# Around the first image pair of a whitening and Fourier-filter kernel: order of the mask products, banks of the inverse column transform, statistics of the second pair, idle products around the factor

## The chip, the cores and the metric

The kernel runs on one core of one Trainium2 chip. The metric is device time in microseconds (us), the median of several runs. Engines are named as in the profile: PE is the matrix engine, DVE the vector engine, ACT the scalar engine, POOL the general engine, SP the queue that starts transfers.

## The reference, cut to what matters

The input is `x`, 16 images of 56 x 56 positions with 64 channels, fp32. First a whitening over all positions, then one block of a Fourier network:

```python
f = x_flat - mean(x_flat); ff = (1-EPS) * f @ f.T / (n-1) + EPS * I      # 64 x 64
L = cholesky(ff); x = solve_triangular(L, I) @ f * gamma + beta
h = layer_norm(x, n1_g, n1_b)
xf = rfft2(h)                                   # per image, over both axes
o1 = relu(complex block product of xf with w1, + b1)   # 8 blocks of 8 channels
o2 = softshrink(complex block product of o1 with w2, + b2, 0.01)
h = irfft2(o2) + h + x
out = gelu(layer_norm(h, n2_g, n2_b) @ mw1 + mb1) @ mw2 + mb2 + h
```

## The kernel before

The 16 images are worked in 8 pairs; a pair is 112 rows (2 images x 56) by 3584 values. The instructions of each engine are one list in a fixed order, written out by hand, with semaphores between the engines.

**Head, once.** `covariance` builds the 64 x 64 Gram matrix from all pairs as they arrive. `factor` eliminates it column by column: 63 steps that go PE to DVE to PE. In each step PE also issues `keep_streaming`, small products whose result nobody reads. After the last step PE issues two products of one row by 512 columns (`beta_rows(5)` and `beta_rows(6)`, which put beta into two PSUM banks), then the transpose of the whitening matrix; DVE copies that to `wy`.

**First pair before its transforms.** PE whitens pair 0 in seven chunks (`whiten`, L986), ACT copies each to `ybuf` (L1370), and DVE in `first_h` takes statistics of each (`stat_w`, L582, `bn_stats`). Then comes the chain `mean_rstd` (15 small operations, L602 on), and the normalisation (L802, L804, and 16 operations of ACT, L1375). After that `first_h` adds beta to pair 1 out of seven banks (`ev_whiten(1, ...)`, L666), multiplies the block weights by their masks (`masked_weights`: four products for `w1s`, L572, two for `w2s`, L575; both inputs lie in SBUF), and takes six of the eight parts of pair 1's statistics.

**A step (`step(i)`), once per pair.** On PE: `dft_h` (L1001), `dft_w` (L1011), `layer_1` (L1026, reads `w1s`), `layer_2` (L1042), `inv_w` (L1053), `inv_h` (L1066). Between these PE has the second half of pair i-1 (the two layers with gelu, L1088 and L1097) and the whitening of pair i+1; in step 0 there is neither, so PE has nothing to put into a wait. DVE adds the biases of layer 2 (L686) and clamps (L692), POOL subtracts (`shrunk_sum`, L424). For the next pair DVE does statistics, `mean_rstd`, `ln1_subtract` (L643) and `ln1_rstd` (L649); it adds the result of `inv_h` to the residual in `ev_inv_h` (L714), eight chunks, and takes statistics of the sum (`ln2_stats`, then `ln2`, L627). POOL also has three long operations for each pair on SBUF data: `begin_residual` (L406), and in `add_h` a scaling (L411) and a sum (L414).

**Banks.** `inv_h(i, k)` writes two chunks, `FIN + 2k` and `FIN + 2k + 1`, to banks 1 and 2, for every k. `free_b` makes it wait until the chunks before have been read, by DVE. Banks 4 to 7 belong to the gelu layer of pair i-1 at that time; in step 0 they are empty. The next `dft_h` writes bank 1 first, and so waits for DVE to have read `FIN + 6`.

In step 0 the list of DVE is: layer 1's share, layer 2, statistics parts 6 and 7 of pair 1, `mean_rstd`, the four halves of L643 and L649, then `ev_inv_h(0, ...)` in pairs with `ln2_stats(0, 0..3)` between the last ones.

Of the kernel before, what the change touches and what calls it, by code (L numbers as in the profile page):

```python
# [29 lines left out]
B, H, W, C = 16, 56, 56, 64  # L30
# [6 lines left out]
ROWS = 2 * H  # L37
FREE = W * C
WP = W // 2
# [34 lines left out]
def b_done(who, k):  # L74

    return sum(who in readers for readers in B_READERS[:k + 1])
# [16 lines left out]
def before_in_bank(banks):  # L93

    last = {b: k for k, b in enumerate(banks)}
    out = []
    for k, b in enumerate(banks):
        out.append((last[b], k <= last[b] and b not in banks[:k]))
        last[b] = k
    return out  # L100
# [8 lines left out]
ORDER = (4, 0, 1, 2, 3, 5, 6, 7)  # L109
WHITEN = (BANK_X,) * 5 + (1, 2)  # L110
B_BEFORE = before_in_bank(B_BANK)


def mlp_order(i):
# [55 lines left out]
def build(nc, x, consts, params, out):  # L170
# [5 lines left out]
    with ExitStack() as ctx:  # L176
# [156 lines left out]
        with nc.Block() as block:  # L333
# [110 lines left out]
            def _(dve):  # L444
# [262 lines left out]
                def ev_inv_h(i, ks):  # L707
                    for k in ks:
                        if k == 0:
                            dve.wait_ge(r_ready, i + 1)  # L710
                        dve.wait_ge(pe_b, i * B_CHUNKS + FIN + k + 1)
                        q, h, c2 = k // 4, k // 2 % 2, k % 2
                        r = rf[i % 2].rearrange("p (w d j h) -> p w d j h", j=CH // 2, d=2, h=2)[:, q * WP:(q + 1) * WP, c2, :, h]
                        nc.vector.tensor_tensor(r, bank[B_BANK[FIN + k]][0:ROWS, 0:7 * C].rearrange("p (w j) -> p w j", w=WP),  # L714
                                                r, ALU.add).then_inc(b_dve, 1)

                def ln2_stats(i, k):
# [6 lines left out]
                def step(i, ahead, behind):  # L724
                    def slice_(s, e0, e1, e2, e3):

                        e0()
                        e1()
                        e2()
                        if behind and s > 0:  # L730
                            ev_mlp(i - 1, s - 1)
                        e3()

                    def next_(what, *args):
                        if ahead:
                            what(i + 1, *args)

                    def whitened_next(*ks):
                        if i > 0:
                            next_(ev_whiten, ks)  # L740

                    def stats_next(*parts):
                        next_(ln1_stats, [q for q in parts if i > 0 or q >= 6])

                    if behind:
                        ln2_stats(i - 1, 4)
                        if i > 1:
                            ev_mlp(i - 2, SLICES - 1)
                        for k in range(5, 8):
                            ln2_stats(i - 1, k)  # L750
                        ln2(i - 1)
                    if i > 0:
                        next_(ev_whiten, [1])
                    ev_layer_1(i)
                    if i == 0:
                        folded_weights()
                    slice_(0, lambda: whitened_next(2, 3, 4), lambda: whitened_next(5),
                           lambda: whitened_next(6), lambda: stats_next(0))
                    slice_(1, lambda: ev_layer_2(i, [0]), lambda: (ev_layer_2(i, [1]), stats_next(1)),
                           lambda: ev_layer_2(i, [2]), lambda: (ev_layer_2(i, [3]), stats_next(2)))  # L760
                    slice_(2, lambda: (ev_layer_2(i, [4]), stats_next(3)),
                           lambda: (ev_layer_2(i, [5]), stats_next(4)),
                           lambda: ev_layer_2(i, [6]), lambda: (ev_layer_2(i, [7]), stats_next(5)))
                    slice_(3, lambda: stats_next(6, 7), lambda: next_(mean_rstd, 0),
                           lambda: next_(ln1_subtract, 0), lambda: None)
                    slice_(4, lambda: next_(ln1_rstd, 0), lambda: next_(ln1_subtract, 1), lambda: None,
                           lambda: next_(ln1_rstd, 1))
                    slice_(5, lambda: ev_inv_h(i, [0, 1]), lambda: None, lambda: ev_inv_h(i, [2, 3]), lambda: None)
                    if ahead:
                        slice_(6, lambda: ev_inv_h(i, [4, 5]), lambda: (ln2_stats(i, 0), ln2_stats(i, 1)),  # L770
                               lambda: ev_inv_h(i, [6, 7]), lambda: (ln2_stats(i, 2), ln2_stats(i, 3)))
# [17 lines left out]

                def first_h():  # L790

                    for k in range(7):
                        dve.wait_ge(whitened, k + 1)
                        last = stat_w(ybuf, range(8 * k, 8 * k + 8))
                    last.then_inc(ln_step[0], 1)
                    mean_rstd(0, 0)
                    late, early = slice(Y0_DVE, W), slice(0, Y0_DVE)
                    nc.vector.scalar_tensor_tensor(small[:, 4, late], small[:, 0, late], -1.0, small[:, 3, late],
                                                   ALU.mult, ALU.mult).then_inc(h0_shift, 1)
                    y4 = ybuf[:].rearrange("p (w j h) -> p w j h", j=CH, h=2)  # L800
                    mean, rstd = (small[:, j, early].unsqueeze(2).unsqueeze(2).broadcast_to((ROWS, Y0_DVE, CH, 2)) for j in (0, 3))
                    nc.vector.tensor_tensor(h_tok[:, early], y4[:, early], mean, ALU.subtract).then_inc(h0_sub, 1)  # L802
                    dve.wait_ge(h0_sub, 1)
                    nc.vector.tensor_tensor(h_tok[:, early], h_tok[:, early], rstd, ALU.mult).then_inc(norm1_step, 2)  # L804
                    ev_whiten(1, range(7))
                    masked_weights()
                    ln1_stats(1, range(6))

                covariance_and_factor()
                first_h()  # L810
# [7 lines left out]
            def _(pe):  # L818
# [60 lines left out]
                def keep_streaming(k):  # L879

                    for part in ((0, C), (C, 0), (C, C)):
# [2 lines left out]
                        nc.tensor.matmul(t[cols, 128:128 + 128], ident[rows, 0:C], ident[rows, 0:128], start=True, stop=True,  # L884
                                         skip_group_check=True)

                def factor():
                    for k in range(C - 1):

                        j = max(k - 1, 0)  # L890
                        rows = elim[:, j % 2, k:k + C + 1]
                        pe.wait_ge(s_dve, DV_COV + 4 * j)
                        one = nc.tensor.matmul(rowk_ps[k % 2], ident[0:C, k:k + 1].broadcast_to((C, C)), rows,
                                               start=True, stop=(k == 0))
                        if k > 2:
                            keep_streaming(k)
                        if k > 0:

                            pe.wait_ge(s_dve, DV_COV + 4 * j + 2)
                            one = nc.tensor.matmul(rowk_ps[k % 2], ahead_v[:, j % 2:j % 2 + 1].broadcast_to((C, C)),  # L900
                                                   rows, start=False, stop=True)
                        one.then_inc(s_pe, 1)
                        if k == 0:
                            mean_column()
                        if k == 2:
                            pe.wait_ge(s_negm, 2)
                        if 2 < k < C - 2:
                            keep_streaming(k)
                    pe.wait_ge(s_dve, DV_ELIM)
                    for k in (5, 6):  # L910
                        beta_rows(k)
                    pe.wait_ge(s_negm, 2)
                    pe.wait_ge(s_dve, DV_W)
                    nc.tensor.transpose(wt_ps, ediag[:], ident[0:C, 0:C]).then_inc(s_pe, 1)

                def free_b(i, k):

# [129 lines left out]
                def inv_w(i, ks):  # L1047
                    for k in ks:
# [5 lines left out]
                                                    start=True, stop=True)  # L1054
                        last.then_inc(pe_b, 1)

                def inv_h(i, k):

                    q, h = k // 2, k % 2
                    pe.wait_ge(b_act, i * B_ACT + b_done("act", INVW + 4 * h + 3))  # L1060
                    t = [free_b(i, FIN + 2 * k + d) for d in range(2)]
                    for m in range(2):
                        g = g_v[:, m, h, q * WP:(q + 1) * WP, :].rearrange("p w j -> p (w j)")
                        for d in range(2):
                            rows = slice(C * d, C * d + KR)
                            one = nc.tensor.matmul(t[d][0:ROWS, 0:7 * C], cc("invh")[rows, ROWS * m:ROWS * m + ROWS], g[rows],  # L1066
                                                   start=(m == 0), stop=(m == 1))
                            if m == 1:
                                one.then_inc(pe_b, 1)
# [453 lines left out]
```

## Time and profile before

| | |
|---|---|
| median of 3 runs | 830.2 us (829.85, 830.2, 835.94) |
| profiled execution | 835.37 us, its span 833.6 us |
| PE, DVE, ACT, POOL busy | 93%, 70%, 47%, 32% of the span |
| mean granted clock of PE | 0.967 of full |
| chain that ended last | PE 75%, DVE 20%, issue 3% of the span |

The span runs from the first to the last instruction of one execution. Steps 1 to 6 repeat with a period of about 82.9 us. A window's "PEclk" is the share of full clock that PE was granted: 1.00 is 2.4 GHz, 0.50 is 1.2 GHz.

### The profile page before, as it was taken

The numbers are of one execution on the slowest core, as the hardware profiler recorded it, in microseconds if no ns is written. First come the engines' busy times: TensorE is split into PE (matmuls) and PEld (weight loads), VectorE is DVE, ScalarE is ACT, GpSimd is POOL, SyncE is SP. The second block draws the span as 40 slices with busy tenths as digits, with TensorE's granted clock in tenths as the row PEclk, the third lists the DMA queues.
The fourth block names the chain that finished last, engine by engine and source line by source line (L and its number), as shares of the span: only waits on it lengthen the run. The fifth ranks groups of instructions, "written<-read, shape, count | busy, mean of one in ns | idle before, by whom it ended". The sixth has DMA issues, their size and how long they took to land.

```text
span 833.6 us, 18629 instructions
## 1 busy us (share of the span) xinstructions
PE 772.0 (93%) x7537; PEld 533.1 (64%) x7537; DVE 579.4 (70%) x1860; ACT 394.2 (47%) x757; POOL 262.8 (32%) x107
## 2 busy tenths in 40 slices
PE   7988999686899999999999999999999998989987
PEld 5985548555576667666666767676767674756433
DVE  4557988998667677767776767676767686844561
ACT  0011006533275646564656465656555645565455
POOL 4000000923264036403640364036403640373000
PEclk9898988889799999999999999999999999999999
DMA  9954002003000030003100310030001000101012
GB/s 246 250 131 139 4 2 79 1 2 78 1 1 25 22 89 23 25 23 83 30 25 23 81 31 25 23 109 3 25 23 34 1 24 24 34 1 35 23 34 67
DMA packets 10375, 39.50 MB, mean 47 GB/s; under 512 B 1282, under 2 KB 1410, under 8 KB 8834
## 3 DMA queue, kind: packets, MB, share of 16 engines
q1 hardware_dynamic: 10290, 38.31, 16.6%
q8 instruction: 60, 0.98, 0.5%
q14 instruction: 25, 0.20, 0.1%
HBM read 25.46 MB, written 12.85 MB: 46 GB/s over the span
## 4 chain that ended last, share of the span: by engine, by line
PE 75%; DVE 20%; issue 3%; ACT 1%; DMA 0%; DVEq 0%; ACTq 0%
PE psum L1088 10%; PE psum L1097 10%; PE psum L1066 6%; PE psum L1042 6%; PE psum L1053 6%; PE psum L1001 6%; PE psum L1011 5%; PE psum L1026 5%; PE psum L986 5%; PE psum L833 4%; DVE stats L582 3%; PE psum L1106 3%; PE psum L971 2%; DVE w1s L572 2%; PE psum L1079 2%
## 5 line engine op out<-in xcount | busy, mean ns | idle before, releaser
L1287 ACT ACTIVATE hid<-psum,hbias 128x448 f32<-128x448 f32 x224 | 123.9, 635 | 79.5 <-PE psum L1088 79.5
L424 POOL TENSOR_TENSOR p_y<-layer,clamped 128x512 f32<-128x512 f32 x64 | 75.5, 1180 | 92.8 <-DVE clamped L692 92.8
L406 POOL TENSOR_TENSOR rbuf<-ybuf,prm 112x2560 f32<-112x2560 f32 (+2 forms) x7 | 31.8, 4543 | 229.0 <-DVE hbuf L804 134.6
L1088 PE MATMUL psum<-n2T,mw1s 64*128 64x448 f32 x448 | 100.9, 569 | 2.0 <-ACT n2T L1280 2.0
L1097 PE MATMUL psum<-hid,prm 128*64 128x448 f32 x448 | 96.3, 552 | 2.0 <-DVE oslice L701 2.0
L1066 PE MATMUL psum<-u_r,cst 58*112 58x448 f32 x256 | 60.4, 592 | 15.1 <-DVE rbuf L714 10.9
L411 POOL TENSOR_TENSOR hbuf<-hbuf,prm 112x3584 f32<-112x3584 f32 x8 | 49.7, 6213 | 69.0 <-DVE n L627 48.7
L1042 PEld LDWEIGHTS psum<-w2s,o_g 128*64 128x64 f32 x1856 | 60.1, 138 | 15.4 <-issue 10.8
L686 DVE TENSOR_TENSOR layer<-psum,prm 128x512 f32<-128x512 f32 x64 | 40.4, 631 | 41.5 <-PE psum L1042 41.5
L1053 PEld LDWEIGHTS psum<-cst,p_y 128*128 128x128 f32 x512 | 61.2, 192 | 10.6 <-issue 6.2
L1042 PE MATMUL psum<-w2s,o_g 128*64 128x64 f32 x1856 | 66.1, 224 | 1.9 <-issue 1.5
L1053 PE MATMUL psum<-cst,p_y 128*128 128x112 f32 x512 | 66.8, 277 | 0.5 <-DVE layer L686 0.5
L1097 PEld LDWEIGHTS psum<-hid,prm 128*64 128x64 f32 x448 | 27.3, 136 | 58.4 <-issue 42.8
L986 PE MATMUL psum<-wy,xT 128*112 128x128 f32 x448 | 59.8, 286 | 2.7 <-DVE ybuf L666 1.2
L1234 ACT COPY u_r<-psum 112x464 f32<-112x464 f32 x64 | 35.0, 546 | 57.6 <-PE psum L1001 57.6
L986 PEld LDWEIGHTS psum<-wy,xT 128*112 128x112 f32 x448 | 54.0, 185 | 11.5 <-issue 10.6
L1088 PEld LDWEIGHTS psum<-n2T,mw1s 64*128 64x128 f32 x448 | 39.4, 188 | 30.0 <-issue 21.4
L1001 PEld LDWEIGHTS psum<-cst,hbuf 112*112 112x112 f32 x512 | 52.3, 177 | 9.2 <-issue 9.0
L1026 PE MATMUL psum<-p_y,w1s 64*128 64x435 f32 (+1 forms) x256 | 49.3, 533 | 9.4 <-DVE w2s L575 8.8
L1001 PE MATMUL psum<-cst,hbuf 112*112 112x116 f32 x512 | 55.1, 265 | 2.2 <-DVE rbuf L714 1.4
L582 DVE BATCH_NORM_STATS2 stats<-ybuf 112x6 f32<-112x64 f32 x392 | 53.2, 208 | 4.5 <-ACT ybuf L1370 4.3
L1011 PE MATMUL psum<-cst,u_r 112*128 112x116 f32 x464 | 53.4, 276 | 1.3 <-ACT u_r L1234 1.3
(133 smaller groups left out, 1375.7 us busy)
## 6 DMA issues: line engine op xcount, KB each, us to landing
xin<-x_dram SPq DMA_DIRECT2D x8, 1568.0 KB, 9.2
out_dram<-oslice SPq DMA_DIRECT2D x56, 224.0 KB, 2.2
ybuf<-x_dram SPq DMA_DIRECT2D x2, 1568.0 KB, 18.0
fbuf<-x_dram SPq DMA_DIRECT2D x2, 1568.0 KB, 21.1
xin<-x_dram SPq DMA_DIRECT2D x4, 392.0 KB, 5.6
n<-x_dram SPq DMA_DIRECT2D x1, 1568.0 KB, 24.1
n<-x_dram SPq DMA_DIRECT2D x4, 392.0 KB, 17.0
prm<-params_dram SPq DMA_DIRECT2D x1, 742.0 KB, 4.6
```

The costliest lines, as they stand in the source:

```text
L424: nc.gpsimd.tensor_tensor(yk, a, b, ALU.subtract).then_inc(y_ready, 1)
L582: last = nc.vector.bn_stats(stats[:, w, :], src[:, w * C:(w + 1) * C])
L986: last = nc.tensor.matmul(t[0:ROWS, j * 128:(j + 1) * 128], xT[:, w * ROWS:(w + 1) * ROWS], wy[:], start=(i > 0), stop=True, skip_group_ch ...
L1001: last = nc.tensor.matmul(t[0:ROWS, j * 2 * KR:(j + 1) * 2 * KR], h_w[:, 4 * k + j, :], cc("f1", ROWS), start=True, stop=True)
L1011: last = nc.tensor.matmul(t[:, j * 4 * KF:(j + 1) * 4 * KF], u_r[0:ROWS, (4 * k + j) * 128:(4 * k + j + 1) * 128], cc("f2", ROWS), start=T ...
L1026: one = nc.tensor.matmul(t[b][:, 0:(z - a) * KF], w1s[C * b:C * b + C, 256 * s + 128 * half:256 * s + 128 * half + 128], p_v[C * b:C * b + ...
L1042: last = nc.tensor.matmul(t[C * r:C * r + C, j * C:j * C + C], o_g[:, at:at + C], w2s[:, 128 * half + C * r:128 * half + C * r + C], start ...
L1053: last = nc.tensor.matmul(t[:, j * 112:j * 112 + 112], y_v[:, 4 * k + j, :], cc("invw"), start=True, stop=True)
L1066: one = nc.tensor.matmul(t[d][0:ROWS, 0:7 * C], cc("invh")[rows, ROWS * m:ROWS * m + ROWS], g[rows], start=(m == 0), stop=(m == 1))
L1088: nc.tensor.matmul(t[:, 0:4 * ROWS], mw1s[C * v:C * v + C, HH * m:HH * m + HH], n2T[C * v:C * v + C, s % 2, :], start=True, stop=True).the ...
L1097: last = nc.tensor.matmul(t[C * v:C * v + C, 0:4 * ROWS], pp("mw2")[:, C * m:C * m + C], hid[:, s % 2, m, v, :], start=(m == 0), stop=(m = ...
L1287: nc.scalar.activation(hid[:, s % 2, m, v, :], bank[CH_MLP[i].bank[k]][:, 0:4 * ROWS], ACT.Gelu, bias=hbias[:, m:m + 1]).then_inc(c_act, 1)
```

## The change

- `masked_weights()` goes to the start of `first_h`.
- Pair 1's statistics are taken all eight parts at once in `first_h`; step 0 has none of them.
- In step 0 the chunks `FIN + 2` to `FIN + 5` of `inv_h` go to banks 4 to 7, so that only `FIN + 6` and `FIN + 7` wait, for DVE's reading of `FIN` and `FIN + 1`.
- In step 0 DVE adds all eight chunks of `inv_h` first and takes `ln2_stats(0, 0..3)` after them.
- `stream_full(3)`, three products of 128 rows by 64 by 128 columns whose result nobody reads, is issued four times: after the last step of the factor, after each of the two `beta_rows`, and after the transpose.

```diff
+def fin_bank(i, k):
+    return BANK_HID + k - 2 if i == 0 and 2 <= k < 6 else B_BANK[FIN + k]
...
-                        nc.vector.tensor_tensor(r, bank[B_BANK[FIN + k]][0:ROWS, 0:7 * C].rearrange("p (w j) -> p w j", w=WP),
+                        nc.vector.tensor_tensor(r, bank[fin_bank(i, k)][0:ROWS, 0:7 * C].rearrange("p (w j) -> p w j", w=WP),
...
                     def stats_next(*parts):
-                        next_(ln1_stats, [q for q in parts if i > 0 or q >= 6])
+                        if i > 0:
+                            next_(ln1_stats, parts)
...
+                    if i == 0:
+                        ev_inv_h(0, range(8))
+                        for k in range(4):
+                            ln2_stats(0, k)
+                        return
                     slice_(5, lambda: ev_inv_h(i, [0, 1]), lambda: None, lambda: ev_inv_h(i, [2, 3]), lambda: None)
...
                 def first_h():
+                    masked_weights()
                     for k in range(7):
...
                     ev_whiten(1, range(7))
-                    masked_weights()
-                    ln1_stats(1, range(6))
+                    ln1_stats(1, range(8))
...
+                def stream_full(n):
+                    for _ in range(n):
+                        nc.tensor.matmul(bank[7][C:2 * C, 128:256], ident[:, 0:C], ident, start=True, stop=True, skip_group_check=True)
...
                         if 2 < k < C - 2:
                             keep_streaming(k)
+                    stream_full(3)
                     pe.wait_ge(s_dve, DV_ELIM)
                     for k in (5, 6):
                         beta_rows(k)
+                        stream_full(3)
                     pe.wait_ge(s_negm, 2)
                     pe.wait_ge(s_dve, DV_W)
                     nc.tensor.transpose(wt_ps, ediag[:], ident[0:C, 0:C]).then_inc(s_pe, 1)
+                    stream_full(3)
...
+                def free_fin(i, k):
+                    if i > 0 or k < 2:
+                        return free_b(i, FIN + k)
+                    if k >= 6:
+                        pe.wait_ge(b_dve, b_done("dve", FIN + k - 6))
+                    return bank[fin_bank(i, k)]
...
-                    t = [free_b(i, FIN + 2 * k + d) for d in range(2)]
+                    t = [free_fin(i, 2 * k + d) for d in range(2)]
```

## Rows read from the trace of the kernel before

**Rows 1.** The chain that ended last, in order of time: start us, us, what.

```profile
119.90 3.43 PE psum L865 x4
...
124.34 6.74 PE psum L986 x32
...
131.72 4.17 DVE stats L582 x32
...
149.44 18.19 DVE w1s L572 x4
...
192.08 1.87 DVE stats L582 x14
...
220.14 1.91 PE psum L1001 x17
```

**Rows 2.** Timeline, DVE, first pair: last masks (start us, us, what).

```profile
159.71 7.92 DVE L572 TENSOR_TENSOR w1s<-prm,cst 128x128 f32<-128x128 f32 x1
167.55 0.48 DVE L575 TENSOR_TENSOR w2s<-prm,cst 128x128 f32<-128x128 f32 x2
```

**Rows 3.** Timeline, POOL, the same stretch.

```profile
145.40 7.82 POOL L406 TENSOR_TENSOR rbuf<-ybuf,prm 112x3584 f32<-112x3584 f32 x1 [134.62 <-DVE hbuf L804]
...
153.16 6.28 POOL L411 TENSOR_TENSOR hbuf<-hbuf,prm 112x3584 f32<-112x3584 f32 x1
...
159.58 7.90 POOL L414 TENSOR_TENSOR rbuf<-rbuf,hbuf 112x3584 f32<-112x3584 f32 x1
```

**Rows 4.** Timeline, step 0: transform, layer 1, layer 2.

```profile
152.54 6.73 PE L1011 MATMUL psum<-cst,u_r 112*128 112x116 f32 x58 [0.64 <-ACT u_r L1234]
...
168.09 6.21 PE L1026 MATMUL psum<-p_y,w1s 64*128 64x435 f32 x24 [8.81 <-DVE w2s L575]
...
178.88 1.15 PE L1042 MATMUL psum<-w2s,o_g 128*64 128x64 f32 x32 [1.52 <-issue]
```

**Rows 5.** Timeline, step 1: layer 1 and DVE's share of it.

```profile
234.88 5.92 PE L1026 MATMUL psum<-p_y,w1s 64*128 64x435 f32 x32
...
236.69 5.48 DVE L675 TENSOR_SCALAR o_g<-psum,prm 64x435 f32<-64x435 f32 x8 [0.94 <-PE psum L1026]
```

**Rows 6.** Timeline, end of the factor to the second whitening.

```profile
122.60 0.25 DVE L549 TENSOR_SCALAR ediag<-elim,scol 64x64 f32<-64x64 f32 x1
123.26 0.31 PE L914 MATMUL psum<-cst,ediag 64*64 64x64 f32 x1
...
127.17 1.11 DVE L582 BATCH_NORM_STATS2 stats<-ybuf 112x6 f32<-112x64 f32 x8 [3.03 <-ACT ybuf L1370]
...
138.88 6.37 PE L986 MATMUL psum<-wy,xT 128*112 128x128 f32 x56 [0.72 <-ACT xT L1226]
```

**Rows 7.** Windows: span us, PE, PEld, DVE, ACT, POOL busy (times), PEclk, DMA.

```profile
18.00:21.00 3.00, 3.00 (x5) 0.92 (x3) 1.37 (x1) 0.00 (x0) 0.00 (x0) 0.50 1.03 263
...
120.40:123.60 3.20, 3.17 (x5) 0.72 (x3) 2.03 (x13) 0.00 (x0) 0.00 (x0) 0.50 0.00 0
124.40:130.40 6.00, 6.00 (x28) 6.00 (x29) 2.22 (x16) 1.76 (x3) 0.00 (x0) 0.50 0.01 1
...
206.00:219.00 13.00, 9.63 (x24) 3.52 (x24) 4.71 (x20) 0.00 (x0) 7.53 (x2) 0.50 0.00 0
```

**Rows 8.** Timeline, end of step 0: first inverse product, adds, POOL.

```profile
192.24 0.87 POOL L424 TENSOR_TENSOR p_y<-layer,clamped 128x320 f32<-128x320 f32 x1 [0.26 <-DVE clamped L692]
...
199.31 1.76 PE L1066 MATMUL psum<-u_r,cst 58*112 58x448 f32 x8 [0.71 <-ACT u_r L1271]
...
205.47 1.15 DVE L714 TENSOR_TENSOR rbuf<-psum,rbuf 112x448 f32<-112x448 f32 x2
```

**Rows 9.** Timeline, DVE in step 1; then step 2, DVE beside POOL.

```profile
229.82 3.95 DVE L627 TENSOR_TENSOR n<-rbuf,small 112x1792 f32<-112x1792 f32 x2
...
294.69 5.63 POOL L406 TENSOR_TENSOR rbuf<-ybuf,prm 112x2560 f32<-112x2560 f32 x1 [24.57 <-DVE oslice L701]
...
297.69 1.86 DVE L582 BATCH_NORM_STATS2 stats<-fbuf 112x6 f32<-112x64 f32 x14
```

## The prediction

> **What bounds the kernel now.** I began with the page's shares (in the table above): PE is busy nearly all the time and the chain that ended last is mostly PE, with a fifth on DVE. An average like that doesn't say where the fifth lies, so the second view was the chain in order of time. From about 220 us on it is PE with few breaks, in steps that repeat. What the change touches lies ahead of that, between the end of the factor and 220.14, where pair 1's `dft_h` starts. There the chain leaves PE four times [rows 1]: for the end of the factor, for pair 0's statistics, for 18.19 us of `w1s`, and for DVE's work ahead of `inv_h`. After 220.14 PE repeats with the same lists as before, so what is won by that point should be won at the end, and the whole estimate is one question: how much earlier does PE start pair 1's `dft_h`? The third view was the timeline of each engine in that stretch, the fourth the granted clock in windows.
>
> **Part 1, the masks.** Four products of 128 x 128 take 18.19 us as a group [rows 1], yet two products of the same shape right after them take 0.48 us together [rows 2], so 0.24 us each. One of the slow ones lasts 7.92 us and ends at 167.63 [rows 2]; POOL's sum over SBUF ends at 167.48 [rows 3]. The group of four begins at 149.44 in the first of POOL's three operations and ends with the third [rows 1, 3]. So three of the masks each wait out one operation of POOL. It is a lock, not slow arithmetic. At the start of `first_h` POOL has nothing to do until 145.40 [rows 3], and DVE waits 3.03 us for the first chunk of `ybuf` [rows 6]. Six products of 0.24 us are 1.45 us: hidden in that wait. If PE becomes faster there (part 4), the wait shrinks to some 1.8 us and still covers them; with no cover they'd cost 1.45 us. The constants they need were loaded before the factor, so the added wait is no wait.
>
> The Trainium skill has a rule for this ("SBUF — State Buffer", section "Who interferes with whom"): a DVE instruction with two inputs in SBUF contends with a GpSimd instruction that reads SBUF, the second one blocks until the first ends, and one with at most one SBUF input doesn't. The trace agrees, by 7.92 us against 0.24.
>
> **What the masks release.** PE ended `dft_w` at 152.54 + 6.73 = 159.27 and began `layer_1` at 168.09, having waited 8.81 us for the masks [rows 4]. Behind them DVE still had six parts of statistics (42 x 0.13 us, 5.4 us) before its share of layer 1, so layer 1's last bank was read at 178.8 and `layer_2` began at 178.88 [rows 4]. After the change DVE has only the statistics in front of it, now 56: from 149.4 they take 56 x 0.13 = 7.3 us (14 take 1.87, [rows 1]) and end at 156.7, ahead of layer 1. They have one input each, and beside a long POOL operation 14 of them took 1.86 us, as many as without it [rows 9], so POOL's lock shouldn't hold them. Layer 1 then goes as in step 1: PE starts at once, at 159.3, and DVE's last chunk ends (236.69 + 5.48) - 234.88 = 7.29 us after PE's start [rows 5]: 166.6. `layer_2` follows at 166.7 in place of 178.88: **12.2 us**. Next late would be POOL, whose long sum ends at 167.48 [rows 3], before the first subtraction of layer 2 (some 2.5 us after PE's start, 169.2); that subtraction doesn't wait. The price if POOL did bind is bounded by 0 and 1 us.
>
> **Part 2, statistics at one go and inverse transform on six banks.** I count in times of before less 12.2. DVE's last clamp ends at about 192.1 - 12.2 = 179.9. Before, 14 statistics came next (1.87 us, [rows 1]); they are gone, hidden as above. What is left is the chain of `mean_rstd` and the four halves: 205.47 - 193.95 = 11.5 us [rows 1, 8]. So `ev_inv_h` begins at 191.5. One small term against: POOL's last subtraction (0.87 us, [rows 8]) now runs beside `mean_rstd`, which has two inputs in SBUF; it costs between 0 and 0.9 us, and I take 0, because DVE begins first, and put 0.9 into the range.
>
> PE: `inv_h(0, 0)` began at 199.31 and took 1.76 us at full clock [rows 8], behind ACT's copies of `inv_w`, which don't change: now 187.1. The second and third product go to their own banks: 3 x 1.76 us, over by 192.4. PE waits for DVE's first two adds, 1.15 us [rows 8]: 192.7. The fourth product ends at 194.5. DVE adds four more chunks by 192.7 + 4 x 0.58 = 195.0 and `FIN + 6` by 195.6. `dft_h` of pair 1 waits for that one alone: 195.7. Before it was 220.14 - 12.2 = 207.9. **12.2 us**, of which 1.87 are the statistics moved, 1.86 the two parts of `ln2_stats` that stood ahead of `FIN + 6`, some 4.8 the three products that PE ran at half clock (24 halves in 9.63 us, [rows 7]), and the rest the ping-pong on two banks.
>
> What is moved behind: DVE now starts `ln2_stats` about 0.2 us later after `dft_h`'s start and has 56 of them, not 42 (1.8 us more), then `mean_rstd`, one whitening chunk and the two multiplies (3.95 us, [rows 9]). Before, these ended at 233.8 and DVE's share of layer 1 began at 236.69 [rows 5, 9]. Between lay 0.7 us of whitening add and 2.2 us of idle time. The 2.0 us go into that gap and nearly fill it, so I charge nothing, up to 1 us in the range. POOL's `add_h(1)` starts 2 us later for the same reason, and it has more than 6 us of slack before its next subtraction.
>
> **Part 3, the end of the factor.** The two one-row products ended at 123.33 and PE began the transpose at 123.26, while DVE had its operand at 122.85 [rows 1, 6]. At full clock the products would be out of the way; that is 0.3 us. PE ran the whitening of pair 0 at 1.2 GHz: 28 halves in 6 us, against 56 halves in 6.37 us for pair 1 [rows 6, 7]. At full clock a chunk takes 0.91 us (6.37 / 7), at half 1.71, so DVE's first statistics would start 0.8 + 0.3 us before 127.17 [rows 6]: 126.1. From there DVE binds, with 56 statistics at 1.04 us for eight (4.17 for 32). They would end at 133.4 in place of 131.72 + 4.17 = 135.89 [rows 1]. **2.5 us**, if the idle products hold the clock. The whole chain behind it (normalisation, pair 1's transposes on ACT and PE) moves with it.
>
> **Do the idle products hold it?** They take 0.23 us each (28 of that width in 6.37 us), 12 of them 2.7 us; before the transpose there are nine, 2.05 us, beside two one-row products of 0.86 us at full clock (3.43 us for both at half). From 119.1 that ends at about 123.0, just as DVE is ready. So at full clock they cost nothing. [...] If the clock falls anyway by 120.3, as before, nine idle products take 4.1 us and the one-row ones 3.4: PE reaches the transpose at 126, the three last products delay the whitening a little more, and it starts 3.3 us later than before. Both ends: +2.5 and -3.3 us. I take the gain, since the gap of 0.8 us without any product is filled too.
>
> **The sum.** 2.5 + 12.2 + 12.2 = 26.9 us against the profiled execution: 835.37 - 26.9 = 808.5. The median before is 5.2 us lower than that execution. Runs differ in where the half-clock stretches begin and end, and the profiled one paid for three that the change removes (at 120 to 130, at the masks, and the 13 us at 206, [rows 7]). A run with shorter ones has less to win, so I don't subtract the 5.2 again, or only a little: **808**, 2.7% below the median.
>
> **Rivals.**
> - *The idle products fail.* The clock falls and they run at half. [...] Time 808.5 + 5.8 = 814.3; if it falls only near 123, about 811.
> - *More is won.* The 5.2 us lie elsewhere (at 18 to 28 us the clock is low too) and stay won: 830.2 - 26.9 = 803.3.
> - *The lock holds statistics too.* Then 56 of them start at 167.5 and end at 174.8, layer 1's last chunk at 180.2 and `layer_2` at 180.3, 1.4 us later than before: 808.5 + 12.2 + 1.4 = 822.1. Against it: 14 in 1.86 us beside POOL [rows 9].
> - *Slower.* The idle products leave PE at 1.2 GHz for good in the first pair's step. PE has about 60 us of full-clock work between the whitening and pair 1's `dft_h`; at half it takes 120. It decides from 27 us of such work on, and in full gives 808.5 + 60 = 868. Against it: each half-clock stretch before ended once PE was full.
> - *It doesn't do what it says:* that DVE, and not the banks, sets the end of step 0. The sum already has DVE there; if its 11.5 us chain grew by 0.9 and PE then paused long enough for the clock to fall again, it is 3 us: 812.
>
> **How the numbers follow.** Forecast (807 to 809) 0.50; failed idle products (811 to 815) 0.24; the long pause 0.09; more won 0.11; held statistics 0.04; slower 0.02. For 8 in 10 the range takes in the first three, the bound of 1 us for the DVE backlog, and part of the fourth: 802 to 815. A measurement of this kernel can tell about 1% (8 us) from no change: faster needs less than 821.9. Only held statistics and the slower case miss it: faster 0.94, same 0.04, slower 0.02.
>
> **What would show it.** L572's group at some 1 us instead of 18.3, before 126 us. L1026's first group right behind L1011's last. DVE's 56 statistics without a break, over before L1026. PEclk of 1.00 from 119 to 135 (first rival: 0.50). Three L1066 groups of 1.76 us in a row, the fourth after a short pause. L1001's second start near 193.3 instead of 220.14, and from there the old rows moved by 26.9 us. I'd be wrong if PE waits for DVE at pair 1's layer 1, or if the half-clock stretch comes back at `inv_h`.

## The result and the profile after

The changed kernel takes 806.5 us (median of 4 runs, 806.2 to 809.76). The kernel before took 830.9 us on the same chip (829.85 to 835.94, 4 runs). The ratio is 0.968, 95% interval 0.964 to 0.973: 3.2% faster. In two later series of runs the same kernel took 809.7 and 808.2 us against 832.6 and 833.2 for the kernel before (ratios 0.970 and 0.970), so the gain is 23 to 25 us, and 2 or 3 us of a median belong to the series. Three executions in the experiments below took 1121, 1851 and 2473 us; they are left out of every median and ratio, and of the one among them that was profiled (masks alone) only the first 425 us are used, in which its granted clock was like the others'.

The profiled execution of the changed kernel has a span of 808.0 us, 25.6 less than before. The page's chain, by engine:

```profile
PE 84%; DVE 12%; issue 2%; ACT 1%; DMA 0%; DVEq 0%; ACTq 0%
```

The DVE share has gone from 20% to 12%, and `w1s` is no longer in the chain. The chain in order of time says what is left of DVE on the path (start us, us, what); it answers to [rows 1]:

```profile
124.44 7.20 DVE stats L587 x56
...
141.07 6.62 PE psum L1020 x64
...
148.30 6.73 PE psum L1030 x58
155.03 5.90 PE psum L1045 x32
...
175.90 0.85 DVE small L610
...
187.64 3.81 DVE rbuf L719 x7
...
191.59 6.57 PE psum L1020 x64
```

There is no mask in it. PE goes from pair 0's first transform (141.07) to layer 1 without a break, and pair 1's `dft_h` starts at 191.59 instead of 220.14. The timeline of the masks and the statistics, DVE and POOL, answers to [rows 2, 3]:

```profile
121.51 0.90 DVE L577 TENSOR_TENSOR w1s<-prm,cst 128x128 f32<-128x128 f32 x4
...
141.16 7.82 POOL L411 TENSOR_TENSOR rbuf<-ybuf,prm 112x3584 f32<-112x3584 f32 x1 [130.38 <-DVE hbuf L816]
...
145.23 7.19 DVE L587 BATCH_NORM_STATS2 stats<-n 112x6 f32<-112x64 f32 x56
...
154.96 5.92 PE L1045 MATMUL psum<-p_y,w1s 64*128 64x435 f32 x32
...
156.77 5.49 DVE L680 TENSOR_SCALAR o_g<-psum,prm 64x435 f32<-64x435 f32 x8 [4.35 <-PE psum L1045]
```

The four products take 0.90 us instead of 18.2. The 56 statistics run in 7.19 us beside POOL's first two long operations (141.16 to 155.14), 0.13 us each, and are over 4.35 us before DVE is next needed. The end of step 0 answers to [rows 8]:

```profile
175.82 0.93 DVE L610 TENSOR_TENSOR small<-stats 112x56 f32<-112x56 f32 x1
...
182.71 4.77 PE L1093 MATMUL psum<-u_r,cst 58*112 58x448 f32 x24 [0.71 <-ACT u_r L1298]
...
188.94 1.76 PE L1093 MATMUL psum<-u_r,cst 58*112 58x448 f32 x8 [1.46 <-DVE rbuf L719]
```

Three products of `inv_h` run in one go at full clock, and the fourth waits for two adds. L610, the third of `mean_rstd`'s operations, takes 0.93 us instead of 0.25: it has two inputs in SBUF and POOL's last subtraction (175.63 to 176.64) runs beside it.

What the whole comparison comes to is best seen by cutting both traces at the same instructions: the last step of the factor (DVE's last `elim`, which starts at 119.57 before and 116.08 after), the start of `dft_h` for pairs 0, 1 and 7, the start of `layer_2` in step 0, and the end.

| stretch, us | before | after | gain | predicted |
|---|---|---|---|---|
| start to the factor's end | 119.57 | 116.08 | 3.49 | 0 |
| factor's end to pair 0's `dft_h` | 25.74 | 24.99 | 0.75 | 2.5 |
| to `layer_2` | 33.57 | 21.29 | 12.28 | 12.2 |
| to pair 1's `dft_h` | 41.26 | 29.23 | 12.03 | 12.2 |
| to pair 7's `dft_h` | 493.66 | 493.66 | 0.00 | 0 |
| to the end | 119.78 | 122.72 | -2.94 | 0 |

The six sum to 25.6. The three rows in the middle are as forecast to a quarter of a microsecond. The three others (head, end of the factor, end of the kernel) differ between executions of one kernel, in the last two with the clock of PE. The windows of the changed kernel (span us, busy of PE, PEld, DVE, ACT, POOL, PEclk, DMA) answer to [rows 7]:

```profile
116.30:119.40 3.10, 3.09 (x12) 1.28 (x12) 2.54 (x16) 0.00 (x0) 0.00 (x0) 1.00 0.00 0
119.50:122.90 3.40, 3.40 (x16) 2.62 (x15) 1.74 (x8) 0.00 (x0) 0.00 (x0) 0.50 0.01 2
123.00:141.00 18.00, 15.95 (x139) 14.64 (x137) 16.04 (x76) 13.53 (x30) 0.00 (x0) 1.00 0.32 91
710.10:713.30 3.20, 3.20 (x8) 1.28 (x8) 0.00 (x0) 1.16 (x2) 3.20 (x1) 0.50 0.00 0
778.40:781.60 3.20, 3.20 (x11) 1.28 (x8) 0.00 (x0) 1.86 (x4) 0.00 (x0) 0.50 0.02 5
```

In this execution the clock fell at 119.5 in spite of the idle products, and it fell at 710 and at 778, where before there was one such stretch in the last pair, at 796.

### The profile page after: what moved, and what is told of

It is laid out like the page before. It is cut to its first block, busy times and chain, and to the rows that moved or that the text cites. A ratio compares the mean times of both kernels' runs of the same rounds, so it can differ in the third digit from the quotient of the medians.

```text
span 808.0 us, 18673 instructions
## 1 busy us (share of the span) xinstructions
PE 765.6 (95%) x7561; PEld 531.2 (66%) x7561; DVE 561.5 (69%) x1860; ACT 393.7 (49%) x757; POOL 263.1 (33%) x107
## 4 chain that ended last, share of the span: by engine, by line
PE 84%; DVE 12%; issue 2%; ACT 1%; DMA 0%; DVEq 0%; ACTq 0%
PE psum L1115 11%; PE psum L1124 11%; PE psum L1020 7%; PE psum L1061 7%; PE psum L1030 6%; PE psum L1072 6%; PE psum L1045 6%; PE psum L1093 5%; PE psum L1005 4%; PE psum L844 4%; PE psum L895 3%; PE psum L1133 3%; PE psum L990 3%; DVE stats L587 2%; PE psum L1106 2%
## 5 line engine op out<-in xcount | busy, mean ns | idle before, releaser
L1115 PE MATMUL psum<-n2T,mw1s 64*128 64x448 f32 x448 | 102.7, 576 | 1.7 <-ACT n2T L1307 1.7
L1093 PE MATMUL psum<-u_r,cst 58*112 58x448 f32 x256 | 55.2, 551 | 8.3 <-DVE rbuf L719 4.1
L1005 PE MATMUL psum<-wy,xT 128*112 128x128 f32 x448 | 57.1, 277 | 1.9 <-DVE ybuf L671 1.2
L1005 PEld LDWEIGHTS psum<-wy,xT 128*112 128x112 f32 x448 | 51.3, 177 | 10.9 <-issue 10.0
L411 POOL TENSOR_TENSOR fbuf<-ybuf,prm 112x2560 f32<-112x2560 f32 (+1 forms) x6 | 24.4, 4075 | 93.8 <-DVE oslice L706 93.8
```

Of the source, the lines that this page charges most:

```text
L411: nc.gpsimd.tensor_tensor(r3, y3, row("b1", ws.stop - ws.start), ALU.add).then_inc(r_begun, 1)
L1005: last = nc.tensor.matmul(t[0:ROWS, j * 128:(j + 1) * 128], xT[:, w * ROWS:(w + 1) * ROWS], wy[:], start=(i > 0), stop=True, skip_group_ch ...
L1115: nc.tensor.matmul(t[:, 0:4 * ROWS], mw1s[C * v:C * v + C, HH * m:HH * m + HH], n2T[C * v:C * v + C, s % 2, :], start=True, stop=True).the ...
```

## Experiments

**The lock.** First the masks alone, in the kernel before:

```diff
                 def first_h():
+                    masked_weights()
...
                     ev_whiten(1, range(7))
-                    masked_weights()
                     ln1_stats(1, range(6))
```

> The kernel before with nothing but the mask products moved to the start of first_h. Lock theory: the four w1s products take 0.9 us together, layer 1 starts as soon as the transform is done, and layer 2 comes 12.2 us earlier after dft_h's start (33.6 us before); two parts of statistics and the two-bank ping-pong stay, so the gain is 12 us: 818 to 820. Rival 'the products are slow by themselves' (18 us of work for DVE wherever they stand): they take 18 us ahead of the first statistics, and the time is above 830.

It took 820.7 us (runs of 815.2, 820.7 and 820.8) against 834.4 for the kernel before in that series: 0.981, 0.977 to 0.985. That is 0.7 above the range given. `dft_h` of pair 0 to `layer_2` took 21.29 us, the same as in the changed kernel to the hundredth, and from there to pair 1's `dft_h` 38.13 (why this is 3.1 less than before is said under the banks). The masks alone are half of the gain, as the lock theory has it.

That they are short at another place doesn't yet say what held them at the old one. The next kernel leaves DVE's list alone and shortens POOL's three operations for pair 0 to one column of 56 each (the residual and the scaled sum of pair 0 lack the other columns):

```diff
-                begin_residual(0, slice(0, W))
-                add_h(0)
+                begin_residual(0, slice(0, 1))
+                pool.wait_ge(pe_b, S2)
+                nc.gpsimd.tensor_tensor(h4[:, :, 0:1], h4[:, :, 0:1], gain[:, :, 0:1], ALU.mult).then_inc(h_scaled, 1)
+                pool.wait_ge(r_begun, 1)
+                pool.wait_ge(h_scaled, 1)
+                nc.gpsimd.tensor_tensor(r4[0][:, 0:1], r4[0][:, 0:1], h_tok[:, 0:1], ALU.add).then_inc(r_ready, 1)
```

> The kernel before, masks in their old place, but POOL's three long operations for pair 0 cover one column of 56 instead of all (pair 0's residual and its scaled sum are left out for the rest, so its output lacks them). Lock theory: nothing else is touched on DVE, and the four w1s products fall from 18.2 us to about 1 us, layer 1 starts 8.8 us earlier and layer 2 about 10 us earlier. Rival 'the products wait for their operands or are slow': they still take 18 us.

The timeline of that kernel, POOL and DVE:

```profile
140.97 0.32 POOL L406 TENSOR_TENSOR rbuf<-ybuf,prm 112x64 f32<-112x64 f32 x1 [130.18 <-DVE hbuf L808]
...
144.92 0.89 DVE L576 TENSOR_TENSOR w1s<-prm,cst 128x128 f32<-128x128 f32 x4
```

The same four products in the same place take 0.89 us once POOL is out of the way, layer 1 follows the transform at once, and `dft_h` to `layer_2` is again 21.29 us: 12.28 less than before, where about 10 were expected. The stretch behind it stays at 41.25, as before. One execution, 820.7 us. So POOL's operations held the masks; neither their operands nor their arithmetic did.

**Are the two parts independent?** The changed kernel with the masks back in their old place:

```diff
                 def first_h():
-                    masked_weights()
...
                     ev_whiten(1, range(7))
+                    masked_weights()
                     ln1_stats(1, range(8))
```

> The changed kernel with the mask products back behind the second pair's whitening. Lock theory: 18 us of masks again, then 56 statistics instead of 42 ahead of layer 1's evacuation (1.8 us more), so 12 to 14 us above the changed kernel: 818.5 to 821, with the end of step 0 still the short one (29.2 us from layer 2 to pair 1's dft_h). Rival 'the two parts are not independent': above 823 or below 817.

It took 822.4 us (819.3 to 824.2), 834.4 for before: 0.985, 0.982 to 0.988. The masks take 18.28 us again and `dft_h` to `layer_2` is 35.37 us, 14.08 more than in the changed kernel: 12.28 for the lock and 1.8 for 14 statistics that now wait behind it. `layer_2` to pair 1's `dft_h` stays at 29.26. The two parts add up. (The time lies 1.4 us above the range given, in a series in which the kernel before was 3.5 us slower than with the first result.)

**The banks.** The changed kernel with two banks for `inv_h` in step 0:

```diff
 def fin_bank(i, k):
-    return BANK_HID + k - 2 if i == 0 and 2 <= k < 6 else B_BANK[FIN + k]
+    return B_BANK[FIN + k]
```

and `free_fin` as `free_b`.

> The changed kernel with the inverse column transform of step 0 on two banks again; the order of DVE and the statistics stay as changed. Theory 'the banks carry most of part 2': the second product waits for DVE's first adds, PE has stood idle by then, the clock is at half, and layer 2 to pair 1's dft_h takes 39 to 41 us instead of 29.2; 816 to 818. Rival 'the moved statistics carry it': 31 to 33 us, 808 to 811.

It took 818.0 us (814.9 to 821.6), 832.6 for before: 0.981, 0.976 to 0.987, as the banks theory has it. Its timeline in step 0, DVE and PE:

```profile
188.06 1.15 DVE L719 TENSOR_TENSOR rbuf<-psum,rbuf 112x448 f32<-112x448 f32 x2
189.35 3.33 PE L1089 MATMUL psum<-u_r,cst 58*112 58x448 f32 x8 [4.47 <-DVE rbuf L719]
192.69 1.16 DVE L719 TENSOR_TENSOR rbuf<-psum,rbuf 112x448 f32<-112x448 f32 x2 [3.48 <-PE psum L1089]
193.99 3.33 PE L1089 MATMUL psum<-u_r,cst 58*112 58x448 f32 x8 [1.30 <-DVE rbuf L719]
...
202.73 6.57 PE L1020 MATMUL psum<-cst,hbuf 112*112 112x116 f32 x64 [0.77 <-DVE rbuf L719]
```

Here PE and DVE take turns: 3.33 us of PE at half clock, then 1.16 us of DVE. `layer_2` to `dft_h` is 39.97 us, 10.7 more than with six banks. In this order of work the banks are most of the 12.0 us. The rest, 41.26 - 39.97 = 1.3 us, is the statistics moved: their 1.87 us, less what L610 waits for POOL.

How the 10.7 us divide is shown by the trace of the masks alone. Its code for this stretch is that of the kernel before, but its clock was at half for 6.8 us only (from 186.4), where it was for 13.65 before (from 205.6). Its second to fourth product of `inv_h`:

```profile
190.00 3.33 PE L1066 MATMUL psum<-u_r,cst 58*112 58x448 f32 x8 [5.69 <-DVE rbuf L714]
194.63 1.76 PE L1066 MATMUL psum<-u_r,cst 58*112 58x448 f32 x8 [1.31 <-DVE rbuf L714]
197.70 1.76 PE L1066 MATMUL psum<-u_r,cst 58*112 58x448 f32 x8 [1.30 <-DVE rbuf L714]
```

Its stretch is 38.13 us, and the 3.13 less than 41.26 are two products at full clock in place of half, 2 x (3.33 - 1.76). So of the 10.7 us the half clock of three products is 4.7, and PE and DVE taking turns is 6.0. The two parts of `ln2_stats` that stood between the adds cost nothing there: before, they ran from 215.81 to 217.67, beside a product of PE that ended at 219.36.

**The idle products.** The changed kernel with none of them (`stream_full` issues nothing):

> The changed kernel without its twelve idle products. The changed kernel's trace shows the clock at half from 119.5 to 122.9, so that they did not hold it in that run; between the last step of the factor and pair 0's dft_h it took 24.9 us (before: 25.5). Theory 'they gain little': this kernel's median is 0 to 1.5 us above the changed one's 806.5, and the stretch is back at 25.5 us. Rival 'they hold the clock in most runs and the profiled one was unlucky': 2 to 3 us above, 808.5 to 809.5. Rival 'they cost time': below 806.

It took 809.9 us (806.6 to 811.9, 6 runs), before 834.4: 0.970, 0.967 to 0.973. The time lies above all three of the ranges given, which had been counted from the first series' 806.5; as a ratio it is no difference from the changed kernel that runs can show (0.968 to 0.970 in three series). The traces show one. PE at the end of the factor, first this kernel, then the changed kernel in its third series, where the clock held:

```profile
115.61 1.97 PE L876 MATMUL psum<-beta_row,one_row 1*112 1x512 f32 x4 [0.81 <-DVE elim L540]
118.71 0.21 PE L932 MATMUL psum<-cst,ediag 64*64 64x64 f32 x1 [1.13 <-DVE ediag L554]
119.69 3.73 PE L1005 MATMUL psum<-wy,xT 128*112 128x128 f32 x16 [0.77 <-DVE wy L560]
```

```profile
117.19 0.87 PE L901 MATMUL psum<-cst 128*64 128x128 f32 x6
118.00 1.11 PE L876 MATMUL psum<-beta_row,one_row 1*112 1x512 f32 x2
119.03 0.87 PE L901 MATMUL psum<-cst 128*64 128x128 f32 x6
119.83 0.24 PE L932 MATMUL psum<-cst,ediag 64*64 64x64 f32 x1
120.00 0.87 PE L901 MATMUL psum<-cst 128*64 128x128 f32 x6
120.85 2.41 PE L1005 MATMUL psum<-wy,xT 128*112 128x128 f32 x20
```

The factor ends at 115.28 in the first and 115.83 in the second. Without idle products the whitening starts 4.41 us after it, and the clock is at half from 118.9 to 125.7. With them it starts 5.02 to 5.05 us after, in every trace of this fill in which the clock holds: a group of three takes 0.80 us from start to the next start, and a beta product 1.03, so that DVE had the transpose's operand at 119.11 while PE came to it at 119.83. They cost 0.6 us and give back 2.4 when the clock holds (25.30 against 23.48 in the table). Whether it held differed between executions of the changed kernel:

| kernel | clock fell between the factor and pair 0's `dft_h` | factor's end to `dft_h`, us |
|---|---|---|
| before; no idle products; short POOL; masks alone | in 4 of 4 traces | 25.74, 25.30, 25.25, 24.70 |
| the changed kernel's fill, 5 traces (masks late and two banks among them) | in 2 | 24.99, 24.98; held: 23.55, 23.49, 23.48 |
| full-height beta products | in 1, later, at 132.3 | 24.43 |
| tuned fill, 3 traces | in none | 22.86, 22.87, 22.86 |

The third row is the changed kernel with beta added by products of 112 rows instead of one:

```diff
+                    pe.wait_ge(s_prm, 16)
                     for k in (5, 6):
-                        beta_rows(k)
+                        nc.tensor.matmul(bank[FIRST_WHITEN[k]][0:ROWS, :], pilot_w[:, 0:ROWS],
+                                         pp("beta", ROWS).unsqueeze(1).broadcast_to((ROWS, 8, C)), start=True, stop=False, ...)
                         stream_full(3)
```

> The changed kernel, but the last two one-row products are made of 112 rows of ones over 112 against beta on 112 partitions: the same sum, all rows at work. Theory 'one-row products do not count for the clock, idle products do': the clock now stays at full from the factor through the whitening in every run, and factor end to pair 0's dft_h takes 22.5 to 23 us instead of 24.9: 804 to 805. Rival 'what lets the clock fall is the pauses, or any short product': no change, 806.5. Rival 'wider products delay the transpose': above 807.

It took 806.8 us (805.6 to 808.3), 3.1 less than the kernel without idle products in the same series; 0.967, 0.964 to 0.969 of before, an interval that overlaps that kernel's. The clock held through the factor and the first whitening, and then fell in the transposes of pair 1, where PE waits for ACT again and again (window of that kernel):

```profile
115.80:132.20 16.40, 14.83 (x109) 11.55 (x109) 13.79 (x92) 8.13 (x14) 0.00 (x0) 1.00 0.01 1
132.40:135.60 3.20, 3.20 (x17) 3.20 (x16) 3.10 (x5) 2.30 (x7) 0.00 (x0) 0.50 0.92 260
```

So neither the expected 22.5 to 23 us (24.43) nor the 804 to 805 us was reached, for a second place in the way.

**A fill that fits.** Full-height beta products, four idle products behind both, two behind the transpose, two ahead of pair 1's whitening. With it went the changed kernel again:

> The changed kernel with the two beta products at full height, four idle products behind both instead of three behind each, two instead of three behind the transpose, and two ahead of pair 1's whitening, where an earlier run lost the clock. Theory 'in the changed kernel three idle products take 0.80 us, so that they end 0.7 us after DVE has the transpose's operand, and the fill has to fit': whitening starts 4.3 us after the factor's end instead of 5.0, the clock holds to pair 0's dft_h, 22.8 to 23.0 us in all, and the median is 1 to 2.5 us below the changed kernel's in this call. Rival 'runs differ by more than this is worth': no difference that can be measured.

> The changed kernel again, to stand beside the others of this call on one chip. Both theories: 805.5 to 810. The time from the factor's end to pair 0's dft_h is what differs from run to run: 23.6 us where the clock holds, 25 us where it falls.

Tuned: 806.5 us (805.2 to 807.9; 0.968, 0.963 to 0.972); the changed kernel 809.7 (804.8 to 810.7; 0.970, 0.966 to 0.974); before 832.6. The whitening starts 4.41 us after the factor's end, as without any idle product, and the clock holds throughout:

```profile
117.20:139.70 22.50, 20.75 (x162) 17.44 (x161) 20.25 (x100) 13.53 (x30) 0.00 (x0) 1.00 0.26 73
```

22.86 us from the factor's end to `dft_h`, inside the 22.8 to 23.0 that were expected. In the median the two are 3 us apart, but the intervals of their ratios overlap; the next series has both again.

**What is given back at the end.** From pair 7's `dft_h` to the end, the same instructions took 119.8 us before and 122.7 after. One more kernel has idle products at four waits of PE in the last pair (bank 0 and bank 7, which are free there), and the two others stood beside it:

```diff
+                    if last_pair(i):
+                        idle(BANK_X, 5)
                     pe.wait_ge(b_act, i * B_ACT + b_done("act", L2 - 1))
...
                         transpose_n(i - 1, 0)
+                    if last_pair(i):
+                        idle(BANK_X, 2)
...
+                    if i == PAIRS - 2 and s == 0:
+                        idle(BANK_X, 3)
...
                 def last_mlp(i):
+                    idle(7, 4)
                     transpose_n(i, 0)
                     transpose_n(i, 1)
+                    idle(7, 2)
```

> The tuned fill, and idle products also at four places of the last pair where PE waits (16 in all: 7 around the layer 1 to gelu turn, 3 in the first gelu slice, 6 around the last transposes). Theory 'the 3 us that the changed kernel gives back after pair 7's dft_h are two half-clock stretches that begin in such waits (709 and 767 to 778 us)': both go, and from pair 7's dft_h to the end it is 119.5 to 120 us instead of 120.7 to 123.6; median 1 to 2.5 us below the tuned fill's. Rival 'idle products get in the way there': 121 or more with no half-clock stretch, median above.

> The tuned fill again, on the same chip as the one above and the one below: 805 to 808 if its 3 us below the changed kernel were real, 809 or more if they were the run's.

> The changed kernel a third time, beside both: 806 to 810, above the tuned fill by 1 to 3 us; rival: no difference between them.

Medians: 805.8 us with the fill in the last pair, 805.1 for the tuned fill (0.967, 0.962 to 0.971) and 808.2 for the changed kernel (0.970, 0.966 to 0.974); before 833.2. So the tuned fill lies where its own theory had it (805 to 808) and again 3 us below the changed kernel. The intervals overlap here too, but of all pairs of one tuned and one changed run the tuned one was the shorter in 25 of 30 in the first series and in 26 of 30 in the second: the 2 to 3 us are probable, not proven. The windows of the fill in the last pair show no half-clock stretch from 709 to 806:

```profile
120.30:142.80 22.50, 20.71 (x162) 17.45 (x161) 20.28 (x99) 13.54 (x30) 0.00 (x0) 1.00 0.24 73
709.00:806.00 97.00, 88.51 (x698) 48.97 (x696) 41.59 (x127) 51.91 (x95) 18.12 (x10) 1.00 0.11 34
```

and its last stretch is 119.76 us, as expected. Over all traces that stretch goes by when the clock falls, counted from pair 7's `dft_h` (at 713.80 before and 685.25 after):

| half-clock stretches begin at, us after pair 7's `dft_h` | kernels | last stretch, us |
|---|---|---|
| none | fill in the last pair | 119.76 |
| 82.1 to 82.4 | before; short POOL; tuned, second series; the changed kernel's third series | 119.78, 119.77, 119.77; 120.58 |
| 25.1 to 25.3 and 83.1 to 83.3 | full-height beta; tuned; masks late | 120.78, 120.72, 120.57 |
| 24.6 to 24.8 and 92.9 to 93.0 | after; no idle products; two banks | 122.72, 122.74, 123.42 |
| 25.8 (6.8 us long) and 94.0 | the changed kernel again | 123.59 |

What each fall costs is read from DVE, whose instructions in this stretch are the same in all these kernels. Laid against those of the tuned fill's second trace (one fall, at 82.4), DVE's instructions of after are late by 1.30 us from 34 on, stay so for more than 50 us, and are late by 2.93 from 97 to the end. The second step lies between these two instructions, in after and then in the tuned fill:

```profile
775.36 2.02 DVE L632 TENSOR_TENSOR n<-fbuf,small 112x1792 f32<-112x1792 f32 x1
782.01 0.69 DVE L706 TENSOR_TENSOR oslice<-psum,fbuf 112x512 f32<-112x512 f32 x1 [4.62 <-PE psum L1133]
```

```profile
776.04 2.02 DVE L632 TENSOR_TENSOR n<-fbuf,small 112x1792 f32<-112x1792 f32 x1
781.05 0.69 DVE L706 TENSOR_TENSOR oslice<-psum,fbuf 112x512 f32<-112x512 f32 x1 [2.98 <-PE psum L1136]
```

They are 6.65 us apart in the first and 5.01 in the second. So the fall near 25 costs 1.3 us and the one near 93 costs 1.6; together they are the 2.94 that were given back. The fall near 82 is free: DVE's times are the same with it and without any fall (the fill in the last pair). The third group of the table agrees: with a fall near 25 and one near 83 DVE is late by 0.8 to 1.0 us from 34 to the end. (The 6.8 us long fall at 25.8 cost 2.1.) The 0.8 us more of the changed kernel's third series (120.58), and 0.7 of the 123.42 of two banks, lie behind the last product and the last addition; they are no fall of the clock, and their cause is open. Each fall begins in a wait of PE or up to 1.0 us behind one, and where it begins differs between executions of one kernel. The fill in the last pair takes the falls away, but in the median it isn't the faster (805.8 against 805.1), though 1 to 2.5 us had been expected.

## Why the prediction was right

The forecast was 808 us, in a range of 802 to 815, and 806.5 was measured. Point by point:

- **The masks (12.2 us).** 12.28. The lock, its cover (DVE's wait ahead of the first chunk, in which they take 1.4 us in all), statistics that run beside POOL, and layer 1 as in step 1 all came out. The short-POOL kernel turned the reading of the three ends into a proof.
- **The end of step 0 (12.2 us).** 12.03. The bound of 0 to 0.9 us for POOL's last subtraction was taken at 0, because "DVE begins first". It was wrong: DVE's first operation of the chain begins first (175.48), POOL's subtraction begins at 175.63, and L610, the third, ends only after it, 0.93 us long instead of 0.25. From the last clamp's end to the first add it took 12.08 us, not 11.5. That it hardly shows in the sum is because the adds came closer together than I had them (3.81 us for seven; by my terms 4.05). The split was wrong where the sum was right: the 4.8 us for PE at half clock hold (4.7), but the statistics moved were worth 1.3 and not 1.87, the two parts of `ln2_stats` nothing and not 1.86, and PE and DVE taking turns 6.0 us, where my split leaves 3.7. That these errors cancel is luck.
- **What is moved behind (nothing).** From pair 1's `dft_h` to pair 7's 493.66 us in both. The two microseconds did go into the gap.
- **The end of the factor (2.5 us).** 0.75. This is the step that failed, in its size and in "at full clock they cost nothing". Where the clock held (the changed kernel's third series), PE still came to the transpose 0.72 us after DVE had its operand. From its first beta product to the transpose PE took 3.67 us (116.16 to 119.83); by my terms it would be 3.1. A beta product takes 1.03 us from start to the next start, not 0.86, which makes 0.34 for two, and an idle product 0.27 us, not the 0.23 of the whitening's products, which makes 0.24 for six. (The first group of three costs nothing: with or without it the first beta product starts 0.33 us after the factor's end.) The clock then fell at 119.5 in the profiled execution and in one other trace of five. The case sat between my forecast and the rival that the idle products fail. The price for failure was too high: the whitening was to start 3.3 us later than before, and started 1.5 later (6.23 us after the factor's end against 4.77), since the clock fell near 119.5 to 120.2, when most of the fill was done. It came back by 123 to 124, where before it stayed at half to 130.5.
- **The head (nothing).** 3.49, of which 2.96 lie ahead of the factor: DVE's first read of the Gram matrix was at 63.61 before and at 60.65 after, in code that didn't change. Over all thirteen traces the factor's end lies between 115.1 and 120.2 us.
- **The end (nothing).** -2.94, by two falls of the clock, near 710 and 778. The page of before showed one dip of the clock in the last pair, near 796, and I didn't ask what one at another place would cost.

Head and end nearly cancel (+0.55), and that is luck. The rule for the median, not to subtract the 5.2 us that the profiled execution of before lay above it a second time, gave 808. By the table, 24.3 us of gain that repeats from trace to trace (12.28 + 12.03), plus 0.75 to 2.3 for the factor's end, against the 830.9 to 833.2 of before in the three series of the changed kernel, gives 804 to 808; they took 806.5, 808.2 and 809.7, one of them 1.5 us outside.

## What to carry to other kernels

A group of tiny vector operations that takes microseconds may be a wait, as here: lay the other engines' rows beside it before blaming its arithmetic, and put two-input SBUF work of the vector engine where the general engine is idle. Where a stage of the first iteration has nothing to overlap with, buffers that belong to the missing neighbour are free, and using them is worth the wait times the number of turns. Idle products are bought with the time at which the next real product is ready: size the fill to end there by the times from start to next start in the trace, of the idle products and of the real ones between them. The kernels whose filler was full height kept the clock at that place in 4 of 4 traces. And cut two traces at the same instructions before believing a sum: here 3.5 us of head came from code that didn't change, and 2.9 us of tail from where the clock fell.

## What the runs showed that I had not expected

- `dft_h` to `layer_2` is 21.28 or 21.29 us in ten traces and 21.20 in the eleventh that has the masks out of the way; pair 1's `dft_h` to pair 7's is 493.6 or 493.7 in all but one (495.8 with short POOL, not explained), while the head differs by 5 us between executions of the same code.
- Two products of one row by 512 columns ran at full clock at 115.6 us in 1.97 us together (no idle products), and at half clock in 3.43 [rows 1]. Whether the clock fell behind them was 4 of 4 without idle products, 2 of 5 with them, and 0 of 4 at full height in that place. That is few traces, and the full-height products also read other weights, and in three of the four another number of idle products stood around them; that the number of rows is the cause wasn't told apart. The rows of before don't tell it either: the clock stood at half through 3.2 us of one-row products and through 6.0 us of whitening behind them alike [rows 7].
- A fall of the clock costs by what it hits: 3.4 us at 1.2 GHz cost nothing near 82 us after pair 7's `dft_h`, 0.8 to 1.3 us near 25, and 1.6 near 93.
